# One more wait per group in a row scatter of a routed expert layer

## The reference

```python
x = x + align(ctx, layernorm(x))   # dynamic time warping: cost matrix, cumulative cost,
                                   # backtracked path; ctx rows are added where the path goes
x = x + ffn(layernorm(x))

# ffn: 16 experts, of which each token takes 2 (top 2 of 4 groups, then top 2 experts)
h = silu(xf @ We1[e] + be1[e]) * (xf @ We3[e] + be3[e])
y = sum over the token's 2 experts of weight * (h @ We2[e] + be2[e])
z = silu(xf @ ws1 + bs1) * (xf @ ws3 + bs3) @ ws2 + bs2     # shared part, every token
out = y + z
```

## Time and profile before

| | |
|---|---|
| median of three executions | 491.47 us (491.30 to 491.77) |
| the profiled execution | 491.77 us, of which 489.9 us lie between its first and last instruction (span) |
| PE, DVE, ACT, POOL busy | 71%, 77%, 34%, 32% of the span |
| mean granted TensorE clock | 0.786 of full speed |
| scatters of line 553 | 64, from 205.8 to 297.3 us; mean of one 997 ns |
| DMA | 69.09 MB, mean 141 GB/s |

### The profile page before, as it was taken

How to read it: one execution, slowest core, us unless ns; L and a number is a source line. 1 busy time by engine, 2 the same in 40 slices (tenths; PEclk the granted TensorE clock), 3 DMA queues, 4 the chain that set the end, 5 groups by cost and what they waited for, 6 DMA issues and landing times.

```text
span 489.9 us, 10676 instructions
## 1 busy us (share of the span) xinstructions
PE 346.8 (71%) x2315; PEld 260.9 (53%) x2316; DVE 374.8 (77%) x2096; ACT 167.2 (34%) x403; POOL 155.3 (32%) x180
## 2 busy tenths in 40 slices
PE   5850100008996188659786997999999999998981
PEld 4750000008995053324544554888788888884550
DVE  4958999999999739794988763566676767772997
ACT  3654000002122011353445310666555666661110
POOL 8000100000000000175757672255555555563000
PEclk9995555555555575557797999899999999999996
DMA  8504897990001000032322397355455545543993
GB/s 327 195 5 116 261 305 156 199 321 7 26 1 53 25 25 1 11 108 78 107 78 105 132 206 247 86 157 153 131 154 137 153 126 145 142 133 116 391 392 133
DMA packets 48343, 69.09 MB, mean 141 GB/s; under 512 B 10470, under 2 KB 38572, under 8 KB 46639
## 3 DMA queue, kind: packets, MB, share of 16 engines
q1 hardware_dynamic: 41407, 51.76, 36.1%
q0 software_dynamic: 6864, 16.86, 9.9%
q10 hardware_dynamic: 32, 0.02, 0.0%
HBM read 39.33 MB, written 31.24 MB: 144 GB/s over the span
## 4 chain that ended last, share of the span: by engine, by line
PE 46%; DVE 41%; ACT 5%; DMA 3%; issue 3%; SPq 1%; DVEq 0%; ACTq 0%
PE psT L999 14%; PE psT L913 9%; PE psT L1009 6%; DVE xk L1451 5%; DVE V L1201 4%; PE psD L989 4%; DVE R L1169 4%; PE psD L884 3%; DVE M L1175 3%; DVE A L1207 3%; DVE F L1167 2%; DVE mask L1197 2%; DVE M L1165 2%; DVE A L1208 2%; PE psC L929 2%
## 5 line engine op out<-in xcount | busy, mean ns | idle before, releaser
L560 POOL DMA_INDIRECT results<-ys,idx x79 | 77.7, 983 | 72.1 <-DVE ys L1419 43.9
L999 PE MATMUL psT<-xsT,w_now 128*128 128x128 f32 x632 | 88.0, 283 | 1.5 <-issue 0.5
L999 PEld LDWEIGHTS psT<-xsT,w_now 128*128 128x128 f32 x632 | 77.5, 193 | 6.4 <-issue 3.0
L553 POOL DMA_INDIRECT slot_rows<-stage,slot x64 | 63.8, 997 | 53.3 <-DVE slot L1338 35.0
L913 PE MATMUL psT<-x2T,sw 128*128 128x512 f32 x128 | 59.2, 613 | 0.6 <-DVE ys L1419 0.6
L823 PE MATMUL psT<-ident,xk 128*128 128x128 f32 x64 | 15.3, 425 | 61.7 <-DMA xk<-in_x 61.7
L1009 PE MATMUL psT<-w,hgT 128*128 x158 | 48.8, 391 | 0.7 <-DVE hgT L1438 0.7
L1438 DVE SCALAR_TENSOR_TENSOR hgT<-psT,w,sg 128x128 f32<-128x128 f32 x79 | 27.7, 351 | 25.8 <-ACT sg L730 23.8
L721 ACT ACTIVATE w_now<-w 128x256 f32 x79 | 32.9, 417 | 40.5 <-PE psD L989 40.3
L823 PEld LDWEIGHTS psT<-ident,xk 128*128 128x128 f32 x64 | 13.8, 242 | 61.7 <-issue 61.7
L540 POOL IOTA tile_no<- 128x79 f32 x1 | 0.2, 215 | 127.1 <-PE psT L862 127.1
(11 more groups left out here) (223 smaller groups left out, 715.3 us busy)
## 6 DMA issues: line engine op xcount, KB each, us to landing
xs<-slot_rows SPq DMA_DIRECT2D x79, 129.0 KB, 2.3
back<-results SPq DMA_DIRECT2D x8, 1024.0 KB, 6.9
slot_rows<-fill SPq DMA_DIRECT2D x32, 129.0 KB, 5.1
xc<-in_x SPq DMA_DIRECT2D x4, 1024.0 KB, 8.8
xk<-in_x SPq DMA_DIRECT2D x4, 1024.0 KB, 12.6
out<-xk SPq DMA_DIRECT2D x8, 512.0 KB, 6.1
w<-in_L_ffn_We SPq DMA_DIRECT2D x1, 2048.0 KB, 12.9
b<-in_L_ffn_be SPq DMA_DIRECT2D x1, 2048.0 KB, 12.6
```

What stands on the lines that cost most here:

```text
L553: pool.indirect_dma_start(out=slot_rows, out_offset=bass.IndirectOffsetOnAxis(ap=slot[:, w, T:T + 1], axis=0), in_=stage[:, T, :], in_offs ...
L560: pool.indirect_dma_start(out=results, out_offset=bass.IndirectOffsetOnAxis(ap=idx[:, u:u + 1], axis=0), in_=ys[:, u, :], in_offset=None, ...
L999: mm = pe.matmul(psH[c % 2][:, lo:lo + P], w_now[:, c % 2, k, lo:lo + I], xsT[:, c % 2, k, :], start=(k == 0), stop=(k == KC - 1))
```

## The change

In POOL's scatter loop the wait for all scatters issued so far, which stood ahead of every eighth tile, stands ahead of every fourth: at T = 4, 8, 12, 16, 20, 24 and 28, and so also in the middle of each group.

```diff
             for T in range(TILES):
                 pool.wait_ge(routed, T // GT + 1)
                 pool.wait_ge(staged, T + 1)
-                if T and T % GT == 0:
+                if T and T % 4 == 0:
                     for w in range(2):
                         pool.wait_ge(scattered[w], 16 * T)
```

## The result

The changed kernel takes 499.96 us in the median of four executions (499.48 to 500.84) against 491.38 us (491.10 to 491.77): a ratio of 1.0166, 95% interval 1.0132 to 1.0200. The direction was as predicted; the size was not. The forecast was 494.7 us, the range ended at 497.5. Seventeen more executions of the changed kernel on record lie between 496.37 and 501.21 us.

A forecast was written before the change was run, and what follows sets the result against it. The shared addition on DVE, ending at 305.43, bounds the loop's start, POOL's last scatter a close second. Lateness 2.4 plus clock 0.8 makes 3.2 us on 491.77, 494.97; for the median 494.7 us, range 492.3 to 497.5.

The forecast's parts named there:

- from that landing to the first tile: From the fourth group's last landed scatter over SP's read and xs load to TensorE's first expert tile: 304.8 to 308.05.
- clock: TensorE at the expert loop's start: after idling it begins at 0.50 of its clock, costing +0.8 us.
- From the releasing event to the start of the scatter POOL takes 0.27 us: POOL's restart in the scatter loop, added to a 2.6 us landing: 2.87 us from scatter to scatter at a wait.
- the cover: At group ends, the start-to-start gap beyond the 2.87 us a landing needs: 1.33, 1.36 and 1.02 us absorb delay.
- Three of the four added waits thus cost 1.1 us together: Added waits in the first three groups: 1.60 us each, partly taken back at group ends, so the fourth starts 1.1 late.
- The landing in the fourth group: The fourth group's 8th scatter, issued at 287.3 amid SP's fills and the bias load: taken to land in 5.5 us.
- high bound of 6.3: Upper case for the fourth group's 8th scatter: a 6.3 us landing, part of a high total of 498.4 us.
- The last landing: The fourth group's 16th scatter, issued about 302 with other traffic nearly over: lands in 2.8 us instead of 5.8.
- half the delay: Fourth group's end: 5.6 us late at the source but landing only 2.65 later, the difference being time now spent queueing.
- no change: Rival, 11%: the wait only moves queueing from the DMA queue to POOL; 492.1 us.
- The slack: Before the loop: the last scatter could land 0.28 us later without delaying TensorE's first tile.
- much slower: Rival, 11%: the fourth group meets fills and biases for its whole length, landings 6.3 and 5.8 us; 498.4 us.

The follow-up runs named there:

- The two kernels with one part each: Changed kernel with only the fourth group's added wait, 492.89 us (ratio 1.0033), and with only the other three added waits, 494.49 us (1.0053, both against the kernel before).
- the one with the small load: Changed kernel with the output bias load cut to a sixteenth (128 KB instead of 2 MB): 497.10 us.
- the control: Kernel before the change with the output bias load cut to a sixteenth: 490.64 us, ratio 0.9988.

## Why the prediction was wrong

The mechanism was the right one: the steps it named are in the trace, in its order. Terms of the sum were too small, above all POOL's restart behind a landing. Times of the changed kernel below are less the 0.40 us by which its routing stage started later.

| term | predicted | measured |
|---|---|---|
| 8th to 9th scatter, groups 1 to 3 | 2.87 us each | 3.25, 3.31, 3.27 |
| 16th to the next group's 1st | 2.87 us each | 3.46, 3.66, 4.25 |
| fourth group starts | 276.5 | 280.7 |
| its 1st to 8th scatter | 10.8 us, as before | 9.2 |
| its 8th to 9th | 5.8 us | 7.8 |
| 16th issued | 302.0 | 306.6 |
| 16th lands | 304.8 | 309.3 |
| from that landing to the first tile | 3.24 us | 2.81 |
| first tile turned | 308.05 | 312.1 |
| clock | +0.8 us | about +0.5 |

The first tile is 4.0 us later than predicted and the clock costs 0.3 us less. That leaves 1.5 of the 5.2 us by which the profiled execution missed the forecast for it (500.17 against 494.97): 0.40 is the later start of the stage, 0.9 lies outside the span, 0.1 comes in the loop and tail. No run tells whether the change has a part in these.

**"From the releasing event to the start of the scatter POOL takes 0.27 us" is the step that failed.** I took that from a release by DVE's cast and used it behind a landing, which none of my rows showed. Behind a landing it is 0.80 us, at six waits ahead of the fourth group: 6 x 0.53 = 3.2 of the 4.2 us by which that group started later than predicted. Both sides of a group end suffer: the wait in the middle is longer, and the cover shrinks from 1.33 to about 0.75 us. "Three of the four added waits thus cost 1.1 us together" hung on a few tenths in each of six steps, and I did not bound the restart from above; the result stores, 0.86 us and more behind what they wait for, stood in the same trace. The remaining microsecond is mostly landings above the 2.6 us of the median (3.46 ahead of the fourth group) and a few scatters of over 0.96 us. The landings are ordinary draws: rows 8 have up to 4.2, but before the change nobody waited for them, and now seven waits do.

**The landing in the fourth group** was mis-sized too, as a consequence. I had 5.5 us for an issue at 287.3, just ahead of the bias load; it was issued at 290.34, just behind the load's own issue at 289.90, and took 7.0. The two kernels with one part each and the one with the small load show this coupling: 4.2 us at 285.9, 7.0 at 290.3, 5.0 at 291.1 with little load. My high bound of 6.3 was the landing of the wrong moment.

**What went against it.** The scatters of the fourth group went out in 9.2 us instead of 10.8, since two of them no longer take 1.99 and 1.87 us (mean of all 64: 975 ns, not 997). In both kernels DVE has an operation of two inputs and 1264 elements at about 278 and another at 280 (lines 1391 and 1394). The two slow scatters ran beside them; the late group misses the first and meets the end of the second with one scatter of 1.29 us. I had left this out.

**The last landing** was right: 2.69 us for the 2.8 taken. What it saves was right in size, not as a share: the last scatter goes out 10.6 us later and lands 7.5 later (0.4 of both is the execution's own), so 3.1 us are time saved in the queue, where 3.0 had been booked; "half the delay" it is not. The rule of the Trainium skill cited there, "DMA: Bandwidth & Descriptors", section "Queues, rings and completion order", can't be judged by it, as the bias load had landed at 300.7 by then. The estimate of 2.3 us for a landing by the Trainium skill, "DMA: Bandwidth & Descriptors", section "Anatomy of one DMA", stood below every landing seen (2.4 and more), and the rival "no change", which leaned on it, is out by the result.

**The slack was larger than 0.28 us.** From the last landing to the first tile it took 2.81 us, not 3.24: TensorE used the tile 0.14 us behind its landing, where I had taken 0.46 from the second tile. That tile says nothing of the first: in the trace TensorE's queue reads a number from `etab` until 306.19 and starts the weight load at 306.22. With the change the landing is 7.14 us later and the tile 6.43; with the fourth group's wait alone 1.6 and 0.8. So about 0.7 us of lateness was free, and the prediction booked 0.4 us too much here. That there was slack is borne out by the control: with the small load the last scatter of the kernel before lands about 3 us sooner, and its time doesn't change.

**The clock** cost a little less than was said. From the first tile's transposes to the third tile's matmuls it is 318.72 - 312.51 = 6.21 us, against 311.37 - 305.68 = 5.69 before.

**The rival "much slower"** had the right shape, a fourth group that meets fills and biases for its whole length, and its 498.4 us were nearer than the forecast, but partly by luck: it took 5.8 us for the last landing, which was 2.7, and a fourth group 4.2 us earlier than it came.

## What to carry to other kernels

A wait for the newest transfer costs its landing plus the issuing engine's restart, and it turns every slow landing into a delay; a wait for the block before the last bounds the queue as well and was free here. Read the release time for the event that will release, from a row in which that event does; where there is none, bound it from above as well. When several small delays are summed, follow the last of them to its new place in time: it may meet a transfer that it missed before.

## What was not expected of the hardware

POOL starts an indirect DMA 0.80 us after the landing that it waited for, 0.73 of it behind its own wait instruction, the same at each of the waits quoted above and (0.82) with another engine's relay. It started 0.28 us after DVE's cast when the landing had come over a microsecond earlier, and 0.35 after it when the landing had come 0.45 us before the cast's end.

The fall of TensorE's clock to 0.50 at the loop's start came in the profiled execution of the kernel before (308 to 311) and not in that of the kernel with no waits, whose work ahead of the loop on TensorE is the same. 35 executions of the kernel before, on another chip than the first three, spread from 489.1 to 495.2 us, more than the 0.2% that those had suggested.
